# A transformer layer's front: normalised rows made again where they are used, instead of stored

## The reference

```python
xn = _layernorm(x, axis=-1)               # (x - mean) / sqrt(var + 1e-5)
x = x + attn(xn, Wq, Wk, Wv, Wo, bo) + ffn(xn, ...)
# attn: softmax(causal(q k^T / 8)) v for each head, then Wo and bo
# ffn:  r = sigmoid(xn @ gate_w + gate_b); top 2 of 16, values over their sum
#       xn + mlp(xn, shared) + sum of value * mlp(xn, expert)
```

## Time and profile before

| | us |
|---|---|
| three runs | 1907.0, 1908.99, 1909.49 |
| median of the runs | 1908.99 |
| the profiled execution, span (no time of its own is listed) | 1908.2 |
| front, to the first projection of the stream | 85.34 |
| TensorE busy | 1859.6 (97%) |
| VectorE busy | 1395.7 (73%) |
| ScalarE busy | 1228.4 (64%) |
| GpSimd busy | 1011.2 (53%) |

### The profile page before, as it was taken

How to read it: one execution, slowest core, us unless ns; L and a number is a source line. 1 busy time by engine, 2 the same in 40 slices (tenths; PEclk the granted TensorE clock), 3 DMA queues, 4 the chain that set the end, 5 groups by cost and what they waited for, 6 DMA issues and landing times.

```text
span 1908.2 us, 53283 instructions
## 1 busy us (share of the span) xinstructions
PE 1859.6 (97%) x20422; PEld 1686.8 (88%) x20422; DVE 1395.7 (73%) x4092; ACT 1228.4 (64%) x3354; POOL 1011.2 (53%) x1506
## 2 busy tenths in 40 slices
PE   5899999999999999999999999999999999999998
PEld 2489998989999998999999999999999999899987
DVE  7678887667777667667666776676676788788886
ACT  4566666666666666667666666666666666666664
POOL 0154447676767663343343333433443767676774
PEclk9999999999999999999999999999999999999999
DMA  9644302434343422445445445445443132323222
GB/s 267 207 167 176 141 21 68 140 106 147 112 140 115 142 79 95 137 142 184 154 160 179 145 161 189 149 145 194 156 143 102 57 117 87 103 86 100 90 73 62
DMA packets 158602, 249.91 MB, mean 131 GB/s; under 512 B 27280, under 2 KB 112528, under 8 KB 158352
## 3 DMA queue, kind: packets, MB, share of 16 engines
q1 hardware_dynamic: 134688, 150.79, 24.3%
q0 software_dynamic: 23664, 95.70, 15.3%
HBM read 151.54 MB, written 94.90 MB: 129 GB/s over the span
## 4 chain that ended last, share of the span: by engine, by line
PE 79%; POOL 6%; DVE 5%; issue 3%; ACT 2%; DMA 0%; POOLq 0%; DVEq 0%; SPq 0%
PE d_bank L695 16%; PE d_bank L747 13%; PE d_bank L733 11%; PE d_bank L722 9%; PE d_bank L763 8%; PE d_bank L708 8%; PE d_bank L821 6%; POOL d_probs L1343 5%; PE d_bank L808 3%; DVE d_probs L1017 3%; PE d_bank L779 2%; DVE d_probs_t L1010 1%; ACT d_probs L890 1%; PE d_bank L831 1%; PE d_bank L768 1%
## 5 line engine op out<-in xcount | busy, mean ns | idle before, releaser
L1343 POOL TENSOR_SCALAR d_probs<-d_probs,d_inverse 128x512 f32<-128x512 f32 (+3 forms) x1024 | 563.7, 565 | 705.2 <-DVE d_inverse L1023 704.8
L890 ACT ACTIVATE d_probs<-d_probs,d_bias 128x512 f32<-128x512 f32 (+3 forms) x1024 | 562.7, 553 | 149.3 <-DVE d_bias L1017 148.0
L1017 DVE CUSTOM_DVE_ANT_0 d_probs<-d_bank,mask 128x512 f32<-128x512 f32 (+3 forms) x1024 | 430.1, 485 | 2.8 <-PE d_bank L733 1.8
L695 PE MATMUL d_bank<-d_xnt,wqk_all 128*128 128x512 f32 x1536 | 408.0, 401 | 0.6 <-PEq L146 0.6
L695 PEld LDWEIGHTS d_bank<-d_xnt,wqk_all 128*128 128x128 f32 x1536 | 270.7, 188 | 52.1 <-issue 0.6
L747 PE MATMUL d_bank<-d_probs_t,d_v 128*64 128x128 f32 x5120 | 308.6, 276 | 0.0
L747 PEld LDWEIGHTS d_bank<-d_probs_t,d_v 128*64 128x64 f32 x5120 | 277.7, 137 | 16.8 <-issue 5.0
L733 PE MATMUL d_bank<-d_ks,d_qs 64*128 64x512 f32 (+3 forms) x3072 | 273.9, 323 | 2.6 <-DVE d_qs L1028 1.4
L733 PEld LDWEIGHTS d_bank<-d_ks,d_qs 64*128 64x128 f32 x3072 | 243.4, 186 | 17.5 <-DVE d_qs L1028 1.8
L722 PEld LDWEIGHTS d_bank<-ident_r,d_probs_moved 64*128 64x128 f32 x5120 | 223.9, 135 | 35.1 <-issue 34.7
L722 PE MATMUL d_bank<-ident_r,d_probs_moved 64*128 64x64 f32 x5120 | 240.6, 245 | 10.4 <-POOL d_probs L1343 9.8
(11 more groups left out here) (126 smaller groups left out, 2206.4 us busy)
## 6 DMA issues: line engine op xcount, KB each, us to landing
queued_rows<-d_zeros SPq DMA_DIRECT2D x79, 256.0 KB, 2.4
d_x<-queued_rows SPq DMA_DIRECT2D x79, 256.0 KB, 3.3
routed_rows<-d_y SPq DMA_DIRECT2D x79, 256.0 KB, 2.2
expert_rows<-d_w SPq DMA_DIRECT2D x32, 384.0 KB, 3.1
a_x_in<-in_L_attn_x SPq DMA_DIRECT2D x16, 512.0 KB, 8.1
xn_rows<-a_xn SPq DMA_DIRECT2D x16, 512.0 KB, 4.9
d_normal<-xn_rows SPq DMA_DIRECT2D x32, 256.0 KB, 3.2
d_base<-in_L_attn_x SPq DMA_DIRECT2D x32, 256.0 KB, 3.4
```

Source lines behind the costliest of these rows:

```text
L695: last = pe.matmul(to[:, :], wqk[:, n % PAIRS, "qk".index(kind), wa, k, :], xnt[n // PAIRS % 2][:, xb, k, :], start=first, stop=(k == KD - ...
L890: act.activation(part, part, ACT.Exp, bias=bias[:, i, h:h + 1], scale=-1.0, accum_out=total[which][:, at % 4:at % 4 + 1]).then_inc(exp_don ...
L1017: dve.tensor_tensor_reduce(out=probs[:, i, h, 0:cols], in0=bank(f"s{fill}", u, h)[:, at * P:at * P + cols], in1=mask[:, T - cols:T], scale ...
L1343: pool.tensor_scalar(part, part, inverse[which][:, at % 4:at % 4 + 1], 1.0, ALU.mult, ALU.mult).then_inc(norm_done, 1)
```

## The change

Normalised rows are no longer stored to DRAM. Mean and reciprocal deviation of all 64 tiles of rows stay in SBUF (`mean_var`, `rstd`), the stream loads rows of x, and normalises them there: GpSimd those of `normal`, in place, ahead of its scaling in step 8b + 3 (and batch 0's at the start), VectorE those of `rows`, in place, in steps 15 to 46. In the front GpSimd normalises in place of VectorE, and SyncE's loads wait for it. The gate weights are padded from 16 to 32 columns; the logits of a batch's four tiles go to four strips of 32 rows of one PSUM tile, so that one transpose of 128x128 brings them back.

```diff
@@ stage_a @@
-        gate_w = sb("gate_w", [P, KD, E])
+        gate_w = sb("gate_w", [P, KD, STRIP])
...
             def _(sp):
                 def load_x(b):
                     if b >= DEEP:
-                        sp.wait_ge(xn_done, b - DEEP + 1)
+                        sp.wait_ge(xn_done, (b - DEEP + 1) * QT)
...
-                def store(b):
-                    sp.wait_ge(xn_done, b + 1)
-                    sp.dma_start(dram["xn"][b], xn[b % DEEP][:, :, :]).then_inc(xn_stored[b % DEEP], DMA)
...
                 for b in range(B):
-                    store(b)
...
             def _(pool):
+                def normalise(b):
+                    pool.wait_ge(rstd_done, b + 1)
+                    if b >= DEEP:
+                        pool.wait_ge(xt_ready, (b - DEEP + 1) * KD)
+                    for q in range(QT):
+                        col = b * QT + q
+                        pool.tensor_scalar(xn[b % DEEP][:, q, :], x_in[b % DEEP][:, q, :], mean_var[:, col, 0:1],
+                                           rstd[:, col:col + 1], ALU.subtract, ALU.mult).then_inc(xn_done, 1)
...
+                for b in range(B):
+                    normalise(b)
...
-                    act.activation(al[b % 2][:, :], lg_ps[b % 2][0:E, :], ACT.Copy).then_inc(al_done, 1)
+                    act.activation(al[b % 2][:, :], lg_ps[b % 2][:, 0:P], ACT.Copy).then_inc(al_done, 1)
...
-                def normalise(b):
+                def invert(b):
                     dve.wait_ge(std_done, b + 1)
-                    dve.reciprocal(rstd[b % 2][:, :], std[b % 2][:, :]).then_inc(rstd_done, 1)
...
-                    for q in range(QT):
-                        last = dve.tensor_scalar(xn[b % DEEP][:, q, :], x_in[b % DEEP][:, q, :], mean_var[b % 2][:, q, 0:1],
-                                                 rstd[b % 2][:, q:q + 1], ALU.subtract, ALU.mult)
-                    last.then_inc(xn_done, 1)
+                    dve.reciprocal(rstd[:, tiles_of(b)], std[b % 2][:, :]).then_inc(rstd_done, 1)
...
                     for k in range(KD):
-                        last = pe.matmul(lg_ps[b % 2][0:E, :], gate_w[:, k, :], xt[b % 2][:, k, :], start=(k == 0),
-                                         stop=(k == KD - 1))
+                        for q in range(QT):
+                            last = pe.matmul(lg_ps[b % 2][q * STRIP:(q + 1) * STRIP, 0:P], gate_w[:, k, :],
+                                             xt[b % 2][:, k, q * P:(q + 1) * P], start=(k == 0), stop=(k == KD - 1))
...
-                    for q in range(QT):
-                        last = pe.transpose(lb_ps[b % 2][:, q, 0:E].bitcast(F32R), al_r[b % 2][:, q * P:(q + 1) * P],
-                                            keep["ident_r"][0:E, 0:E])
-                    last.then_inc(lb_ready, 1)
+                    pe.transpose(lb_ps[b % 2][:, 0, :].bitcast(F32R), al_r[b % 2][:, :], keep["ident_r"][:, :]
+                                 ).then_inc(lb_ready, 1)
@@ stream @@
+        ROWS_AT = {(FIRST_SCATTER, 0): [(0, q) for q in range(QT)]}
+        for s in range(1, B):
+            ROWS_AT[FIRST_SCATTER + 2 * s - 1, 1] = [(s, 0), (s, 1)]
+            ROWS_AT[FIRST_SCATTER + 2 * s, 0] = [(s, 2), (s, 3)]
...
-                    sp.dma_start(normal[:, two, :].bitcast(F32), dram["xn"][b, :, two, :]).then_inc(normal_loaded, DMA)
+                    sp.dma_start(normal[:, two, :], x_src[b, :, two, :]).then_inc(normal_loaded, DMA)
...
-                    sp.dma_start(rows[s % 2][:, q, :], dram["xn"][s, :, q, :]).then_inc(rows_loaded[s % 2], DMA)
+                    sp.dma_start(rows[s % 2][:, q, :], x_src[s, :, q, :]).then_inc(rows_loaded[s % 2], DMA)
...
-                    pe.wait_ge(normal_loaded, (b + 1) * 2 * DMA)
+                    pe.wait_ge(normal_made, (b + 1) * QT)
...
+                def standardise(s, q):
+                    dve.wait_ge(rows_loaded[s % 2], (s // 2 + 1) * QT * DMA)
+                    part, col = rows[s % 2][:, q, :], s * QT + q
+                    dve.tensor_scalar(part, part, mean_var[:, col, 0:1], rstd[:, col:col + 1], ALU.subtract, ALU.mult
+                                      ).then_inc(rows_made, 1)
...
             def _(pool):
+                def standardise(b):
+                    pool.wait_ge(normal_loaded, (b + 1) * 2 * DMA)
+                    for q in range(QT):
+                        part, col = normal[:, q, :], b * QT + q
+                        pool.tensor_scalar(part, part, mean_var[:, col, 0:1], rstd[:, col:col + 1], ALU.subtract, ALU.mult
+                                           ).then_inc(normal_made, 1)
...
                     for q in (part * 2 + half_of,):
+                        pool.wait_ge(rows_made, s * QT + q + 1)
...
+                standardise(0)
                 for u in STEPS:
                     b, k = (u + 2) // PAIRS, (u + 2) % PAIRS
+                    if there("n0", u):
+                        standardise((u + 5) // PAIRS)
```

More of the change, by code:

```diff
@@ L55 @@
 FIRST_SCATTER = 15
+STRIP = 32
 def gate_cols(k):
@@ L108, in stage_a, with tiles_of @@
         lb_ps = [pb(f"lb_ps{r}", [P, QT, P]) for r in range(2)]
+        def tiles_of(b):
+            return slice(b * QT, (b + 1) * QT)
         x_loaded = [sem(f"x_loaded{r}") for r in range(DEEP)]
-        xn_stored = [sem(f"xn_stored{r}") for r in range(DEEP)]
         const_loaded, made = sem("const_loaded"), sem("made")
@@ L789, in turn @@
                         for q in range(QT):
-                            last = pe.transpose(to[:, q * P:(q + 1) * P].bitcast(F32R), normal[:, q, k * P:(k + 1) * P],
+                            last = pe.transpose(to[:, q * P:(q + 1) * P].bitcast(F32R), normal_r[:, q, k * P:(k + 1) * P],
                                                 ident[:, :])
@@ L1243, in _ @@
                     route(u, 0)
+                    for item in ROWS_AT.get((u, 0), ()):
+                        standardise(*item)
                     n = tick(u, 0)
```

53 lines of the change are left out of this document (26 added, 27 removed).

## The result

The changed kernel takes 1947.72 us (median of 5 runs, 1945.46 to 1949.39), the kernel before 1908.96 in the same series (1906.79 to 1909.49): a ratio of 1.0209, interval 1.0198 to 1.022. It is slower by 39 us where 17 us of gain were forecast. The profiled executions have spans of 1946.0 and 1908.2 us.

What follows compares the result with a forecast made beforehand. TensorE, 97% busy, was taken to bound the kernel, and transfers then VectorE its front. 1908.2 - 19.5 (front) + 2 (stream start) + 0.5 (VectorE's rows) = 1891.2 us span, forecast 1892 median, range 1885 to 1902.

Steps and rivals of the forecast that it cites:

- GpSimd's price: Front and stream: GpSimd normalises 128x256 at 0.471 us an instruction, 1.9 us a batch, borrowed from its scaling.
- GpSimd in the stream: Stream: sixteen times 1.9 us of new rows on GpSimd; the first 1.1 us late, the other 15 hidden, 0.
- Rival (2): Stream: GpSimd's new rows stand on TensorE's path, all 28.5 us exposed, 1920 if exposed everywhere; chance 0.06.
- The front's 19.5 us: Front: gain from starting the stream at about 65.8 us instead of 85.34, bounds 12.3 to 24.3.
- The ring of the front: Front's last batches: an x buffer's load, moments, reciprocal and GpSimd take 8.05 us per three batches, 2.7 us each.
- rival (1): Front: GpSimd and VectorE hold each other up at SBUF, 4.1 us a batch, 1899 to 1900 in all; chance 0.11.
- Transfers: Front: without the stores, batch 10's moments start at about 42 us instead of 53.56, between 41.2 and 44.2.
- Strips: Front: gate logits as 16 instructions in four strips take 1.0 us a batch against 1.89.
- rival (4): Front: the strips do nothing, logits stay at 1.9 us, 1.8 us less gain, 1894; counted within the forecast's 0.74.
- VectorE's rows: Stream units 15 to 46: 64 normalising instructions, 0.345 us each, 22 us; 0.5 us taken as cost, 22 as bound.
- rival (3): Stream units 15 to 46: VectorE's 22 us are exposed, half giving 1903, all 1914; chance 0.09.
- The start of the stream: 2 us for GpSimd's first rows, 1.1 us late, and TensorE's cold clock together, between 1.1 and 4.4.

Runs made afterwards that it cites:

- e5: The change with GpSimd normalising by multiply and add with a prepared -mean/std, front and stream, instead of subtract and multiply; 1907.13 us.
- e9: e5 with VectorE in the front taking logits four batches at a time and its low halves two batches later; 1899.28 us.
- e1: The change with VectorE instead of GpSimd normalising in the front, the stream as in the change; 1919.73 us.
- e8: The kernel before with the strips for the gate logits alone, rows still stored and VectorE normalising; 1902.98 us.
- e10: e9 with VectorE's first four row instructions split two and two over their unit's halves, first-half ones behind the splits of k and q; 1896.52 us.
- e4: The change with GpSimd's front normalising in another instruction form every two batches, as a price list; 1942.93 us, one run, not used.
- e11: The change with a second list of GpSimd instruction forms in the front, another every two batches; 1938.3 us, one run, not used.
- e3: The change with no normalising on GpSimd, VectorE doing it in front and stream; 1909.14 us.

## Why the prediction was wrong, point by point

**The step that failed is GpSimd's price**: "its scaling of 128x256 costs 0.471 us an instruction in the stream, 1.9 us a batch". It took the shape from the row and not the operation. The row multiplies by a scalar and by 1.0; the new instruction subtracts. Measured: 1.24 us in the front and 1.22 in the stream, 4.9 us a batch. That it is the price, and neither the place nor the number of the instructions, e5 shows: the same 128 in the same places, in the short form, take 40.6 us less. The term stood twice in the sum: in the front, where GpSimd became the bound, and in "GpSimd in the stream", where 1.9 us were to be hidden with 1.5 to spare and 4.9 were not. With the short form that cover holds as forecast: e5 loses 0.6 us among the scatters and 0.4 among the gathers. The Trainium skill ("GPSIMD Engine Reference", 4.1 Engine selection) says that elementwise work belongs on VectorE and that GpSimd is about line rate for one input; against VectorE's 345 ns from start to start, multiply and add takes 1.6 times as long (552), subtract and multiply 3.5 times (1219), so here that holds at best for some operations.

**Rival (2) named the mechanism and its condition**, "a cost of 0.85 us an instruction would do", at 0.06, and priced it at 1920 because it left the front's gain standing. The front's 19.5 us became a loss of 15.8 by the same price, 35 us more; the stream lost 22 us, where this rival had 28.5.

**Had the price been right, the forecast would still have failed.** e5 has nearly that price (0.60) and takes 1907. The ring of the front was drawn without VectorE's logits: "2.7 us a batch" was 5.1 around 45 us, and 3.9 in the five batches for which it was meant (batch 10's moments start at 48.79, batch 15's at 68.15). That is near rival (1)'s 4.1, but not by its mechanism. It named engines in turns over SBUF; what ran was turns over waits in program order, and e9, which only changes when VectorE takes logits and low halves, gains 9.6 us in the front. What is left in e9 is small: the five batches take 3.2 us each (41.87 to 58.10), the rest from there to the stream 11.7 us instead of 10.3, and the stream starts at 69.83 instead of 65.8.

**Transfers**: right. In e9 the moments of batch 10 start at 41.87 us, where the forecast had about 42, and behind a wait for x:

```profile
41.87 1.41 DVE L250 BATCH_NORM_STATS2 a_stats<-a_x_in 128x6 f32<-128x256 f32 x4 [1.20 <-DMA a_x_in<-in_L_attn_x]
```

The gain in time is smaller. With strips and VectorE normalising in both, the front without stores starts the stream at 74.01 (e1) and with them at 80.41 (e8): 6.4 us, less than the 11.4 at batch 10, since VectorE binds next. **Strips**: 16 instructions were put at 1.0 us; they take 1.08 where the transposes beside them take 1.26, and 0.64 where these take 0.87 as in the earlier trace rows. Together with the shorter way back that gave 4.9 us, not the 1.8 of rival (4).

**VectorE's rows**: 64 at 0.345 were 22 us; they are 35.4 us (595 ns each), since beside GpSimd they run slower: in e10 the two of the 64 that overlap no computing instruction of GpSimd take 409 and 415 ns, the others 586 on average. The forecast also misread their place. The two early ones of a batch stand not before the low half of q, with its 2.24 us of idleness, but before that of k, where VectorE idles 0.29 us in the kernel before:

```profile
359.63 0.69 DVE L1028 TENSOR_TENSOR d_ks<-d_bank,d_ks 128x512 fp32r<-128x512 f32 x1 [0.29 <-ACT d_ks L896]
```

Of the 35.4 us, 1.3 us is shown to lie on the path (e9 against e10), of the 0.5 that I took; rival (3) is wrong, most is hidden. (Half of its chance of 0.09 was to lie up to 1905, 0.045, but "faster than 1905.2" counts 0.03 of it.)

**The start of the stream**, 2 us for GpSimd's first rows and the clock: 4.6 in the change, 1.9 with the short form, and 1.4 with the strips alone and nothing new on GpSimd. TensorE's rows take this apart. Up to the second transposes of probabilities e8 runs as before, 16.22 us from the stream's start in both. Then three groups, here before and in e8, differ:

```profile
101.56 0.83 PE L722 MATMUL d_bank<-ident_r,d_probs_moved 64*128 64x64 f32 x16 [2.81 <-POOL d_probs L1343]
102.20 3.60 PE L733 MATMUL d_bank<-d_ks,d_qs 64*128 64x512 f32 x24
105.73 1.72 PE L695 MATMUL d_bank<-d_xnt,wqk_all 128*128 128x512 f32 x6
```

```profile
96.63 1.20 PE L723 MATMUL d_bank<-ident_r,d_probs_moved 64*128 64x64 f32 x16 [2.81 <-POOL d_probs L1344]
97.62 3.81 PE L734 MATMUL d_bank<-d_ks,d_qs 64*128 64x512 f32 x24
101.35 2.52 PE L696 MATMUL d_bank<-d_xnt,wqk_all 128*128 128x512 f32 x6
```

Together they take 1.38 us longer in e8, which is all of its 1.4. The granted clock agrees: from 11 to 31 us after the stream's start it is 0.77 and 0.89 in two stretches of 10 us in e8, 0.83 and 1.00 in the same stretches of before (96 to 116 us), so TensorE spends more of them at 1.2 GHz. Why, behind the same wait of 2.81 us, no run shows. In e5 the same groups take 0.5 us longer than before, and they start 1.4 us later, behind GpSimd's rows and the scaling that these put off: 1.4 where the forecast had 1.1. In the change it is 2.1 us behind GpSimd, 0.5 in these groups, and 2.0 in the first projections, which are longer for the same work (2.90 us instead of 1.62 for the first six instructions) although the granted clock from 102 us on reads 1.00; what lengthens them stays open.

## What to carry to other kernels

A duration may be borrowed from a row only if the operation is the same, not just engine, shape and type; on GpSimd write a normalisation as multiply and add with a prepared -mean/std, never as a subtraction with a scalar. When an engine's work is moved, follow the waits in program order through a whole turn of the loop, with everything that stands between two steps of the same engine, before the slowest engine is taken for the pace. And ask how much room the receiving engine has where it is busiest: 2.2 us of work put 2.3 us later in one unit of eight cost 18 here.

## What the hardware showed that I had not expected

GpSimd's tensor-scalar forms differ by 2.5 times at one shape (0.48 to 1.23 us for 128x256), with every form that subtracts, and an addition alone, on the slow side. One form also differs by place: multiply with 1.0 into another tile took 614 ns in batches 4 and 5 (e4) and 478 in the last two (e11); why, no run shows.

```profile
L201 POOL TENSOR_SCALAR a_xn<-a_x_in,rstd_all 128x256 f32<-128x256 f32 x8 | 3.8, 478 | 0.0
```

VectorE's normalising loses time beside GpSimd: 4.70 us instead of 1.38 in e3. GpSimd's two instructions lose little or nothing there (4.66 and 1.90 us, 4.67 and 1.82 before). I had argued from its length that VectorE's instruction takes no shared path to SBUF; this row speaks against it. The Trainium skill ("SBUF — State Buffer", Who interferes with whom) says that whichever of the two issues first (not VectorE alone, as the forecast had it) has the shared ports for its whole instruction, and a tensor-scalar form can be one that needs them. The first of VectorE's four agrees: it ends at 77.39, just behind GpSimd's first at 77.24. The second does not fit as well: it ends at 80.08, a microsecond behind GpSimd's second (79.10), while GpSimd writes constants.
